# Third convolution of a graph network: marks and hat planes kept in PSUM, with one plane buffer

## The chip, the cores and the metric

The kernel runs on one NeuronCore of a Trainium2 chip. The metric is the device time of one execution in microseconds. It is one program with all its data in that core's HBM at the start; nothing is exchanged with other cores.

## The reference, cut to what matters

A graph of 12,500 nodes and 200,000 edges goes through two blocks, a spline network with three spline convolutions and an attention layer with a gated update. The change touches the third spline convolution alone, the last line of `_L0_gnn_ref`:

```python
def spline_basis(pseudo):                      # pseudo: [E, 3] in [0, 1]
    pos = pseudo * (KS - 1)                    # KS = 5 knots a dimension
    i0 = jnp.clip(jnp.floor(pos), 0, KS - 2).astype(jnp.int32)
    frac = pos - i0
    basis = jnp.prod(jnp.where(combos[None] == 1, frac[:, None, :], 1.0 - frac[:, None, :]), axis=-1)
    ...
def spline_conv(x, row, col, basis, idx, W, b):
    z = jnp.einsum('ni,kio->nko', x, W).reshape(N * K, Fout)       # K = 125
    msg = jnp.einsum('es,eso->eo', basis, z[col[:, None] * K + idx])
    out = jax.ops.segment_sum(msg, row, num_segments=N)
    ...
new_pseudo = jnp.clip(pseudo + t[col] - t[row], 0.0, 1.0)
basis2, idx2 = spline_basis(new_pseudo)
return spline_conv(x, row, col, basis2, idx2, conv_w, conv_b)      # x: 32 features in, 32 out
```

## The kernel before, in words

The program is a chain of phases with a barrier between each two: loading, counting, sorting the edges by source node, a first convolution, the second convolution `flow_conv("c2", ...)`, the third `flow_conv("c3", ...)`, a norm, and the attention. One function, `flow_conv`, builds the second and the third; its argument `moved` is None for the second and the table of node moves for the third. The page and the trace leave buffer and phase numbers out, so both show as `c_...`; the gather from `hid_table` is the second's, the one from `feat_table` the third's.

In the third convolution a node's edges lie together in the array `rows` in HBM, and the nodes are taken in 98 blocks of 128. A block has two halves, `q` = 0 and 1, and a half has 16 windows of 4 nodes. A window is 128 rows of `rows` from where its nodes' edges start. Four strands run side by side, each in its own order:

- **GpSimd (POOL)** fills `rows`. It gathers 128 rows of `feat_table` at a time with an indirect DMA (L961, 1568 of them), whose row numbers it reads from `at` in SBUF; after each four it stores a slot of four tiles to `rows` (L968, 392 stores) and after 16 it copies the next 16 columns of numbers (L956). It never waits for the consumers below.
- **SyncE (SP)** waits until POOL has stored what the block needs (L1012), then, for each half, until VectorE has finished with that half's buffer (L1017), and issues 16 loads of one window each into `rin[:, q]` (L1022) and one of the block's node moves into `trow[:, q]` (L1026).
- **VectorE (DVE)** works on a half in one chain of 19 instructions (`body`, L1108 on). It subtracts the block's first node (`rel`, L1110), makes the edge's position (`pos`, L1123) and the **mark** (L1090), which for each window has, in each of 4 columns, one where the edge belongs to that node. From marks and moves it makes `tsel` (L1128), reduces it to `tsrc` and corrects `pos`. In between and after stand the eight **spreads** (L1084), each mark times feature for two windows. ScalarE makes the sides of the three hats from `pos` (L663 to L668); then DVE finishes the hats (L1144), multiplies the first two dimensions' hats to the **plane** of 5 x 5 values a window (L1095), and plane by third hat to the **basis**, 125 values a window, in two instructions of 8 windows (L1100).
- **TensorE (PE)** multiplies basis by spread for each window into PSUM (L1222), **ScalarE (ACT)** copies the products to `sums` (L1321), and once in two blocks PE mixes the sums with the weights (L1234) and adds up. ACT takes a half's products before it makes the sides of the next half.

Before the change `mark` and `plane` lie in SBUF and have two buffers, one for each `q`. All of PSUM that the third convolution uses is `acc` (four banks of [125, 512]), `mix` and `back` (a bank each); six of the eight banks of 512 fp32 values.

```python
mark = sb(f"{name}_mark", [P, 2, GW2, WN])
plane = sb(f"{name}_plane", [P, 2, GW2, 5, 5])
basis = sb(f"{name}_basis_sb", [P, 2, GW2, 25, 5])
```

Of the kernel before, what the change touches and what calls it, by code (L numbers as in the profile page):

```python
# [13 lines left out]
P = 128  # L14
# [9 lines left out]
WN = 4  # L24
# [30 lines left out]
GW2 = NW // 2  # L55
# [4 lines left out]
def bc(ap, shape):  # L60
    return ap.to_broadcast(shape)
# [14 lines left out]
def allocators(nc, ctx):  # L76
    def sb(name, shape, dt=F32):
        return ctx.enter_context(nc.sbuf_tensor(name, shape, dt))

    def ps(name, shape, dt=F32):  # L80
        return ctx.enter_context(nc.psum_tensor(name, shape, dt))

    def sem(name):
        return ctx.enter_context(nc.semaphore(name))

    return sb, ps, sem
# [782 lines left out]
def flow_conv(nc, c, d, sem, name, turn, table, width, feats, outs, weight, conv_out, moved):  # L869
# [38 lines left out]
    with nc.Block() as block, ExitStack() as ctx:  # L908
        sb, ps, _ = allocators(nc, ctx)
# [1 line left out]
        at = sb(f"{name}_at", [P, 2, RING, slot], U32)  # L911
        rin = sb(f"{name}_rin", [P, 2, GW2, words])
        rel = sb(f"{name}_rel", [P, GW2])
        mark = sb(f"{name}_mark", [P, 2, GW2, WN])
        plane = sb(f"{name}_plane", [P, 2, GW2, 5, 5])
        basis = sb(f"{name}_basis_sb", [P, 2, GW2, 25, 5])
        spread = sb(f"{name}_spread_sb", [P, 2, GW2, feats, WN])
        sums = sb(f"{name}_sums", [K, feats, 2 * P])
# [124 lines left out]
        def _(dve):  # L1043
# [31 lines left out]
            def body(b, item, q):  # L1075
# [16 lines left out]
                                      ALU.is_equal).then_inc(seq, 1)  # L1092

                def make_plane(h):
                    dve.tensor_tensor(plane[:, q, :, :, :], bc(h[:, :, 0, :].unsqueeze(3), [P, GW2, 5, 5]),  # L1095
                                      bc(h[:, :, 1, :].unsqueeze(2), [P, GW2, 5, 5]), ALU.mult).then_inc(seq, 1)

                def make_basis(h):
                    for w in (slice(0, G), slice(G, GW2)):
                        dve.tensor_tensor(basis[:, q, w, :, :],  # L1100
                                          bc(plane[:, q, w, :, :].rearrange("p g a b -> p g (a b)").unsqueeze(3),
                                             [P, G, 25, 5]),
                                          bc(h[:, w, 2, :].unsqueeze(2), [P, G, 25, 5]), ALU.mult)\
                            .then_inc(basis_made, 1)
                        if w.start == 0:
                            dve.wait_ge(basis_made, m * 2 + 1)
# [5 lines left out]
                if moved is None:  # L1112
                    h = rin[:, q, :, src_word + 4:src_word + 19].rearrange("p w (k j) -> p w k j", j=5)
                    make_plane(h)
                    after_step(1)
                    make_mark()
                    after_step(2)
                    make_basis(h)
                    after_step(3)
                    make_spread(*range(pieces))  # L1120
                    dve.sem_inc(seq, 1)
                    return
# [25 lines left out]
                make_spread(6)  # L1148
                after_step(8)
                make_plane(hat[:, q, :, :, :])  # L1150
                make_spread(7)
                after_step(9)
                make_basis(hat[:, q, :, :, :])

            n = dve.value_load(c.passes[0], min_val=1, max_val=EP // P)
# [737 lines left out]
def gnn(nc, ins, out):  # L1893
# [17 lines left out]
    with ExitStack() as top:  # L1911
# [50 lines left out]
        with ExitStack() as nodes:  # L1962
            sb_n, _, _ = allocators(nc, nodes)
            hid = sb_n("hid", [P, NB, HID])
            phase(conv_of_ones, hid[:, :, :])
            phase(conv_to_hidden, "h1", hid[:, :, :], d.stn1_b, d.hid_table)
            phase(flow_conv, "c2", 0, d.hid_table, HID, HID, HID, d.stn2_w, hid[:, :, :], None)
        c.sum3 = sb("sum3", [P, NB, FEAT])
        phase(flow_conv, "c3", 1, d.feat_table, 36, FEAT, FEAT, d.conv_w, c.sum3[:, :, :], d.move)
        c.elr = sb("elr", [P, NB, 2 * HEADS])  # L1970
        c.x, c.h = sb("x2_sb", [P, NB, FEAT]), sb("h2", [P, NB, FEAT])
# [20 lines left out]
```

## Time and profile before

| what | value |
|---|---|
| median of 3 runs | 11174.09 us (11165.35 to 11177.23) |
| span of the profiled execution | 12528.6 us |
| second convolution, 4040 to 6660 us | 2620 us |
| third convolution while POOL gathers, 6670 to 9092 us | 2422 us, POOL busy 1940.1 |
| third convolution after that, to 9620 us | 528 us, POOL busy 0 |
| attention, 9800 to 12528 us | 2728 us |
| DVE busy over the span | 7716.2 us (62%) |
| POOL busy over the span | 7476.5 us (60%) |

The profiled execution is 1354.5 us longer than the median of the timed runs. Its page therefore tells where instructions stand and how long each takes, and less surely how long a phase takes in a run without the profiler. Groups of instructions are given as count, busy time and mean, and behind a bar the engine's idle time just before them with what ended it.

### The profile page before, as it was taken

Reading aid. Unit: us, or ns where it says so; the run is one execution under the profiler, and the core shown is the slowest. Engines: PE = TensorE matmul, PEld = TensorE weight load, DVE = VectorE, ACT = ScalarE, POOL = GpSimd, SP = SyncE. Lnnn points to the kernel's source line nnn. Section 1 sums busy time; section 2 is a strip of 40 time slices with the busy share of each in tenths; the row PEclk is TensorE's granted clock in tenths of the full one; section 3 lists DMA queues with packets and bytes.
Section 4 is the critical chain, followed back from the end, with each engine's and each line's share of the span. In section 5 each row is a group of like instructions: output and inputs, shape, how many; then the busy total and the mean of one; then the engine's idle time right before and its main releaser. Section 6 shows DMA issues by size and latency. Waiting matters only on the chain. (4 is left out here: it accounts for less than half of the span.)

```text
span 12528.6 us, 178083 instructions
## 1 busy us (share of the span) xinstructions
PE 6505.4 (52%) x38968; PEld 5397.9 (43%) x38968; DVE 7716.2 (62%) x17239; ACT 2933.1 (23%) x8407; POOL 7476.5 (60%) x7456
## 2 busy tenths in 40 slices
PE   3466666666475799999994444545555100000000
PEld 2355555555475677777764434434454100000000
DVE  9844444444498676666664444544576267777777
ACT  0011111111132344344432222322343000000001
POOL 5155555655200888888886888888800566666663
PEclk9966666666698999999997667766777555555555
DMA  1210000000733444444443333333322212221221
GB/s 41 65 36 2 2 2 2 2 2 2 14 41 50 93 93 94 92 94 95 92 93 49 50 51 53 54 50 52 54 42 34 35 49 50 51 50 48 51 54 40
DMA packets 1788557, 605.09 MB, mean 48 GB/s; under 512 B 1595943, under 2 KB 1729575, under 8 KB 1788260
## 3 DMA queue, kind: packets, MB, share of 16 engines
q1 hardware_dynamic: 1078132, 311.05, 12.8%
q0 software_dynamic: 255648, 274.30, 10.7%
q10 hardware_dynamic: 454736, 19.28, 3.0%
q8 instruction: 15, 0.25, 0.0%
q14 instruction: 26, 0.21, 0.0%
HBM read 430.75 MB, written 172.95 MB: 48 GB/s over the span
## 5 line engine op out<-in xcount | busy, mean ns | idle before, releaser
L1222 PE MATMUL c_acc<-c_spread_sb,c_basis_sb 128*125 128x256 f32 (+1 forms) x12544 | 2599.2, 376 | 1502.8 <-issue 655.0
L1222 PEld LDWEIGHTS c_acc<-c_spread_sb,c_basis_sb 128*125 128x125 f32 x12544 | 2266.5, 231 | 1803.5 <-issue 1536.3
L1614 POOL DMA_INDIRECT at_ring<-gat_table,at_place x1568 | 1585.7, 1011 | 1188.5 <-issue 1188.5
L609 POOL DMA_INDIRECT rec<-rk_rec,rk_place x1568 | 1619.3, 1033 | 1110.1 <-DVE rk_place L497 620.7
L1321 ACT ACTIVATE c_sums<-c_acc 125x512 f32<-125x512 f32 (+1 forms) x3136 | 1489.3, 490 | 2258.7 <-PE c_acc L1222 1298.6
L961 POOL DMA_INDIRECT c_ring<-hid_table,c_at x1568 | 1707.1, 1089 | 478.9 <-issue 443.2
L961 POOL DMA_INDIRECT c_ring<-feat_table,c_at x1568 | 1602.7, 1022 | 478.1 <-issue 462.9
L1084 DVE TENSOR_TENSOR c_spread_sb<-c_mark,c_rin 128x512 f32<-128x512 f32 (+1 forms) x3136 | 1745.2, 557 | 60.3
L1871 PE MATMUL gr_hps<-ident,gr_hs 128*32 128x128 f32 x98 | 29.8, 408 | 2473.7 <-issue 2066.3
L492 DVE CUSTOM_DVE_ANT_0 rk_junk_l<-rk_look_ps,rk_hi 128x98 bf16<-128x98 f32 x1568 | 402.2, 257 | 1324.1 <-remote 821.1
L1234 PE MATMUL c_mix<-c_sums,c_w 125*64 125x256 f32 (+1 forms) x9408 | 1037.3, 401 | 187.6 <-issue 133.8
L554 PE MATMUL rk_look_ps<-rk_table,rk_lo_t 128*128 128x98 f32 x3136 | 908.7, 425 | 379.5 <-DVE rk_before L492 327.4
L1871 PEld LDWEIGHTS gr_hps<-ident,gr_hs 128*32 128x32 f32 x98 | 6.4, 109 | 2488.1 <-issue 2078.1
L554 PEld LDWEIGHTS rk_look_ps<-rk_table,rk_lo_t 128*128 128x128 f32 x3136 | 705.4, 292 | 503.3 <-DVE rk_before L492 404.2
L1783 DVE TENSOR_REDUCE at_sums<-at_prod 128x128 f32<-128x5248 f32 x98 | 873.3, 8911 | 24.0 <-issue 14.1
L1234 PEld LDWEIGHTS c_mix<-c_sums,c_w 125*64 125x64 f32 (+1 forms) x9408 | 627.4, 132 | 559.2 <-issue 304.0
L530 PE MATMUL rk_rows_ps<-ident,rk_cols 128*128 128x128 f32 x3152 | 771.1, 390 | 4.7 <-ACT rk_cols L564 4.5
L1110 DVE TENSOR_SCALAR c_rel<-c_rin,first 128x16 f32<-128x16 f32 x392 | 103.3, 264 | 1014.6 <-DMA c_rin<-rows 434.9
L587 ACT ACTIVATE rk_table<-rk_run_ps 128x98 f32<-128x98 f32 x784 | 196.2, 250 | 2173.9 <-PE rk_run_ps L549 1208.1
L530 PEld LDWEIGHTS rk_rows_ps<-ident,rk_cols 128*128 128x128 f32 x3152 | 664.9, 292 | 6.4 <-ACT rk_cols L564 6.4
L1144 DVE SCALAR_TENSOR_TENSOR c_hat<-c_hat,c_sides 128x96 f32<-128x96 f32 x196 | 52.5, 268 | 985.3 <-issue 785.6
L487 DVE SCALAR_TENSOR_TENSOR rk_junk<-rk_rows_ps,src_f,rk_earlier 128x128 bf16<-128x128 f32 (+1 forms) x1568 | 647.2, 413 | 2.0 <-PE rk_rows_ps L530 2.0
(356 smaller groups left out, 10126.9 us busy)
## 6 DMA issues: line engine op xcount, KB each, us to landing
c_rin<-rows SPq DMA_DIRECT2D x3136, 42.0 KB
c_rin<-rows SPq DMA_DIRECT2D x3136, 20.0 KB
rows<-c_ring POOLq DMA_DIRECT2D x392, 128.0 KB
rows<-rk_blank SPq DMA_DIRECT2D x112, 252.0 KB
rows<-c_ring POOLq DMA_DIRECT2D x392, 72.0 KB
rows<-at_ring SPq DMA_DIRECT2D x196, 144.0 KB
rec<-rk_rec,rk_place POOLq DMA_INDIRECT x1568
c_ring<-hid_table,c_at POOLq DMA_INDIRECT x1568
```

The lines of the kernel that those rows point to most:

```text
L487: dve.scalar_tensor_tensor(junk[:, u, j // 2, odd:2 * odd + 1, :], rows[:, u, j - odd:j + 1, :], c.src[:, bass.ds(g * G + j, 1)], earlier[ ...
L492: dve.tensor_tensor_reduce(junk_l[:, u, j, :], look[:, j % 2, 0:NB], hi_hot[:, u, j, :], 1.0, 0.0, ALU.mult, ALU.add, before[:, u, j:j + 1 ...
L530: last = pe.matmul(rows[:, u, j, :], bc(cols[:, u, j:j + 1], [P, P]), c.ident[:, :], start=True, stop=True)
L554: pe.matmul(look[:, j % 2, 0:NB], lo_t[:, u, j, :], table[:, k % 2, :], start=True, stop=True).then_inc(looked, 1)
L609: pool.indirect_dma_start(out=d.rec, out_offset=bass.IndirectOffsetOnAxis(ap=place[:, u, j:j + 1], axis=0), in_=rec[:, u, j, :], in_offset ...
L961: pool.indirect_dma_start(out=ring[:, u, j, :], out_offset=None, in_=table, in_offset=bass.IndirectOffsetOnAxis(ap=at[:, h, u, j:j + 1], a ...
L1084: dve.tensor_tensor(spread[:, q, w, :, :], bc(mark[:, q, w, :].unsqueeze(2), [P, 2, feats, WN]), bc(rin[:, q, w, 0:feats].unsqueeze(3), [P ...
L1222: last = pe.matmul(acc[pp % BANKS][:, (w % 2) * WN * feats:(w % 2 + 1) * WN * feats], basis[:, q, w, :, :].rearrange("p a b -> p (a b)"), ...
L1234: last = pe.matmul(mix[k * outs:(k + 1) * outs, 0:2 * P], wsb[:, f, :], sums[:, f, :], start=(i_f == 0), stop=(i_f == each - 1))
L1321: act.activation(sums[:, :, at:at + 2 * WN].rearrange("p f (k n) -> p k f n", n=WN), acc[pp % BANKS][:, 0:pair].rearrange("p (k f n) -> p ...
L1614: pool.indirect_dma_start(out=ring[:, u, j, :], out_offset=None, in_=d.gat_table, in_offset=bass.IndirectOffsetOnAxis(ap=place[:, u, j:j + ...
L1783: dve.tensor_reduce(sums[:, v, :], prod[:, v, :, :, :].rearrange("p s h f -> p (h f) s"), X, ALU.add)\
```

## The change

In the third convolution `mark` and `plane` are allocated in PSUM, and `plane` loses its dimension of two buffers: both halves of a block write and read the same plane. In the second convolution both stay in SBUF, with one plane as well. No instruction is added, removed or moved on any engine.

```diff
-        mark = sb(f"{name}_mark", [P, 2, GW2, WN])
-        plane = sb(f"{name}_plane", [P, 2, GW2, 5, 5])
+        mark = (sb if moved is None else ps)(f"{name}_mark", [P, 2, GW2, WN])
+        plane = (sb if moved is None else ps)(f"{name}_plane", [P, GW2, 5, 5])
...
                 def make_plane(h):
-                    dve.tensor_tensor(plane[:, q, :, :, :], bc(h[:, :, 0, :].unsqueeze(3), [P, GW2, 5, 5]),
+                    dve.tensor_tensor(plane[:, :, :, :], bc(h[:, :, 0, :].unsqueeze(3), [P, GW2, 5, 5]),
                                       bc(h[:, :, 1, :].unsqueeze(2), [P, GW2, 5, 5]), ALU.mult).then_inc(seq, 1)
...
                         dve.tensor_tensor(basis[:, q, w, :, :],
-                                          bc(plane[:, q, w, :, :].rearrange("p g a b -> p g (a b)").unsqueeze(3),
+                                          bc(plane[:, w, :, :].rearrange("p g a b -> p g (a b)").unsqueeze(3),
                                              [P, G, 25, 5]),
                                           bc(h[:, w, 2, :].unsqueeze(2), [P, G, 25, 5]), ALU.mult)\
```

## Rows read from the trace of the kernel before

**Rows 1.** The page: the span.

```profile
span 12528.6 us, 178083 instructions
```

**Rows 2.** Windows by phase: length, busy us (count) by engine, PEclk, DMA share, GB/s.

```profile
core 0: us, PE busy (x) PEld busy (x) DVE busy (x) ACT busy (x) POOL busy (x), PEclk, DMA share, GB/s
...
6670.00:9092.00 2422.00, 1167.36 (x7224) 966.76 (x7224) 1149.66 (x2812) 680.57 (x2136) 1940.10 (x2056) 0.70 0.33 52
9092.00:9620.00 528.00, 309.83 (x2381) 278.58 (x2382) 374.06 (x917) 229.95 (x696) 0.79 (x1) 0.78 0.24 41
```

**Rows 3.** Groups of instructions by line, third convolution while POOL gathers (6670 to 9092).

```profile
L961 POOL DMA_INDIRECT c_ring<-feat_table,c_at x1568 | 1602.7, 1022 | 478.1 <-issue 462.9 <-DMA rows<-c_ring 11.9 <-DMA c_ring<-feat_table,c_at 2.4
L1084 DVE TENSOR_TENSOR c_spread_sb<-c_mark,c_rin 128x256 f32<-128x256 f32 x1184 | 498.2, 421 | 10.2
L1100 DVE TENSOR_TENSOR c_basis_sb<-c_plane,c_hat 128x1000 f32<-128x1000 f32 x294 | 353.7, 1203 | 23.1
L968 POOL DMA_DIRECT2D rows<-c_ring x391 | 313.1, 801 | 0.7
L1095 DVE TENSOR_TENSOR c_plane<-c_hat 128x400 f32<-128x400 f32 x148 | 85.6, 579 | 18.2
...
L1110 DVE TENSOR_SCALAR c_rel<-c_rin,first 128x16 f32<-128x16 f32 x148 | 42.2, 285 | 213.8 <-DMA c_trow<-move 192.1 <-PE c_acc L1222 12.1 <-issue 9.4
L1144 DVE SCALAR_TENSOR_TENSOR c_hat<-c_hat,c_sides 128x96 f32<-128x96 f32 x148 | 39.7, 268 | 945.0 <-issue 785.6 <-ACT c_hat L668 157.2 <-DVE c_spread_sb L1084 2.1
```

**Rows 4.** Line 961 alone: duration in ns, least, median and most.

```profile
L961 POOL DMA_INDIRECT c_ring<-feat_table,c_at x1568: 941/948/1988, 6669.8 to 9086.6; - x196
```

**Rows 5.** Timeline, start and length in us, around one gather of the third convolution.

```profile
8034.13 2.43 DVE L1100 TENSOR_TENSOR c_basis_sb<-c_plane,c_hat 128x1000 f32<-128x1000 f32 x2
8034.19 1.95 POOL L961 DMA_INDIRECT c_ring<-feat_table,c_at  x1 [0.30 <-issue]
```

**Rows 6.** Timeline of the sorting phase, around two indirect DMAs of POOL.

```profile
1803.00 1.68 POOL L609 DMA_INDIRECT rec<-rk_rec,rk_place  x1 [3.40 <-DVE rk_place L497]
...
1803.75 0.97 DVE L465 TENSOR_TENSOR rk_hi<-ramp_bf,src_hi 128x784 bf16<-128x784 bf16 x1
...
1804.98 0.97 POOL L609 DMA_INDIRECT rec<-rk_rec,rk_place  x1 [0.30 <-issue]
...
1805.09 0.48 DVE L487 SCALAR_TENSOR_TENSOR rk_junk<-rk_rows_ps,src_f,rk_earlier 128x256 bf16<-128x256 f32 x1
```

**Rows 7.** Waits of the SP queue in the third convolution: total, times, longest.

```profile
SPq L1017 <- DVE c_spread_sb L1084: 212.0, 30, 21.5
SPq L1012 <- POOLq L972: 32.4, 1, 32.4
```

**Rows 8.** Timeline of SP: three early halves, and two even ones after POOL's end.

```profile
6731.99 9.39 SPq L1022 DMA_DIRECT2D c_rin<-rows  x16
...
6742.80 11.76 SPq L1022 DMA_DIRECT2D c_rin<-rows  x16
...
6757.20 9.69 SPq L1022 DMA_DIRECT2D c_rin<-rows  x16
...
9302.06 9.02 SPq L1022 DMA_DIRECT2D c_rin<-rows  x16
...
9323.98 9.02 SPq L1022 DMA_DIRECT2D c_rin<-rows  x16
```

**Rows 9.** Groups after POOL's end (9092 to 9620).

```profile
L1110 DVE TENSOR_SCALAR c_rel<-c_rin,first 128x16 f32<-128x16 f32 x48 | 11.2, 234 | 77.0 <-PE c_acc L1222 42.3 <-DMA c_trow<-move 34.7
```

**Rows 10.** DVE groups, form by form, whole span: a PSUM input beside SBUF ones.

```profile
L487 DVE SCALAR_TENSOR_TENSOR rk_junk<-rk_rows_ps,src_f,rk_earlier 128x256 bf16<-128x256 f32 x784 | 376.1, 480 | 0.0
L1748 DVE SCALAR_TENSOR_TENSOR at_score<-at_score 128x160 f32<-128x160 f32 x98 | 31.9, 326 | 16.6 <-issue 13.7
L1722 DVE TENSOR_TENSOR gr_gap<-gr_gap,gr_rz 128x64 f32<-128x64 f32 x49 | 11.0, 225 | 1.7
L1718 DVE TENSOR_TENSOR gr_cand<-gr_gps,gr_gap 128x64 f32<-128x64 f32 x49 | 11.0, 225 | 1.7
```

## The prediction

> **What bounds the kernel now.** The change touches the third convolution alone, so I first look for what sets that phase's length. The windows by phase [rows 2] cut it in two: 2422 us in which POOL gathers and stores, then 528 us without POOL. In the first part POOL's own groups leave no hole: 1602.7 us of gathers with 478.1 us between them, 313.1 us of stores [rows 3], in sum 2393.9 of 2422. A gather is followed by the next 0.30 us later, whatever the others do. So POOL waits for nobody, and is itself stretched only by what makes its instructions longer.
>
> Yet POOL does not set the phase's end: 528 us of work are left when it stops. The consumers take 148 halves of blocks (one L1110 each) in the first part [rows 3], 16.4 us a half, and the other 48 [rows 9] at 11.0 us. SP, which feeds them, waits for POOL once, at the start, for 32.4 us [rows 7]. After POOL's end SP starts an even half's loads at 9302.06 and the next at 9323.98 [rows 8]: 21.9 us a block, or 11 a half, and for that stretch the view of SP's waits is empty. So that part is bound by SP's issues of loads. In the first part SP is slower by itself: 25.2 us between the even halves at 6731.99 and 6757.20, with no wait among them (12.6 a half). From 12.6 to 16.4 it is held by the others: VectorE idles 945.0 us before L1144, that is for ScalarE's hats, of which 785.6 us are put down to no cause the profile shows [rows 3], and SP waits 212.0 us for the spreads [rows 7].
>
> **What the change does to POOL.** Two SBUF operands become PSUM operands: the mark in each spread and in the small L1128, the plane in each basis. The rows show why that can matter to POOL. A gather of this line takes 941 ns at least, 948 in the median and 1988 at most [rows 4]. The long ones lie over VectorE instructions with two SBUF inputs: the gather at 8034.19 starts with a basis and takes 1.95 us [rows 5]. In the sorting phase an indirect DMA at 1803.00, with L465 (two SBUF inputs, 0.97 us) begun inside it, takes 1.68; the next, at 1804.98, lies over L487, whose first input is in PSUM and second in SBUF, and takes its 0.97 [rows 6]. L487 has the very arrangement of memories that spread and basis get.
>
> What POOL loses now is the mean over the median: (1022 - 948) ns x 1568 = 116 us [rows 3, 4]. The instructions with two SBUF inputs that remain are the plane (its inputs are hats, only its output moves, 85.6 us), L1144 (39.7 us), the mark's own making and the positions. Spreads and bases are 498.2 + 353.7 = 852 us of the 977 in the four groups named [rows 3], 87%, so some 100 us of the 116 go. I take 100 us: POOL ends after 2322 us in place of 2422.
>
> The Trainium skill says the same mechanism in "SBUF — State Buffer", section Who interferes with whom: a DVE instruction with at most one SBUF input, outside its two-port modes, leaves GpSimd alone, one with two contends with GpSimd's reads. By that rule, the trace agrees: 1.68 against 0.97 us. The page would change nothing in the sum.
>
> **What that is worth at the phase's end.** POOL's end only changes the pace of the consumers from 16.4 to 11.0 us a half. In 100 us less of the first part 100 / 16.4 = 6.1 halves fewer are done; they are done later in 6.1 x 11.0 = 67 us. Net gain: 100 - 67 = 33 us. What hides the other 67 us is SP's queue of loads.
>
> **What it does to VectorE.** No row of the third convolution has a PSUM input. The nearest rows are two. L1718 (first input in PSUM) and L1722 (both in SBUF) are the same instruction at 64 elements, and both take 225 ns: no cost [rows 10]. L1748 takes 326 ns for 160 elements out of SBUF, L487 480 for 256 elements; at the rate by which a basis goes from 256 elements' 421 ns to 1000 elements' 1203 (1.05 ns an element [rows 3]), L487 should take 326 + 96 x 1.05 = 427. So it has 53 ns more, in which its accumulator is contained. Bounds: 0 to +53 ns an instruction. I take 0, since L1718 is the same operation as ours (TENSOR_TENSOR, fp32 out) and L487 is not. Writing PSUM from VectorE is in no row; I take it as equal too, bounded by the same 53 ns, and below nothing by as much, since nothing excludes a faster write.
>
> At the upper bound 13 instructions a half touch mark or plane (mark, tsel, eight spreads, plane, two bases): 13 x 53 = 0.69 us a half, 135 us over 196 halves. Its cover is the wait before L1110, in which VectorE has nothing to do until the loads land: 77.0 / 48 = 1.6 us a half in the second part [rows 9], 213.8 / 148 = 1.44 in the first [rows 3]. Both exceed 0.69, so it costs nothing as long as the loads are late. If that cover is gone, what counts is the ring through ScalarE, below.
>
> Here the skill has a rule against the change. "VectorE: DVE Perf Modes", section The TRN2 errata, gives 58 cycles of fixed cost to an instruction from SBUF and 120 to one from PSUM. That is at 0.96 GHz an estimate of 65 ns more for each of the 11 readers, about 0.7 us a half, and the sum would still be covered. The pair in rows 10 (225 and 225 ns) does not show it.
>
> **One plane buffer.** Both writes and reads of the plane are VectorE's, in its own order: the next half's plane comes after this half's bases, with fifteen instructions between. No wait is added. Cost nothing; there is no other engine behind it. `mark` keeps two buffers. The two banks that they take are beside `acc`, `mix` and `back`, which PE writes.
>
> **The sum.** 12528.6 - 33 = 12496 us for the profiled execution [rows 1]. The timed median is 1354.5 us below that span. I carry the difference over as it is: 11174.1 - 33 = **11141 us**.
>
> **Rivals.** The profiled run may be paced otherwise than the timed ones, and the 785.6 us without a cause before L1144 are the candidate: if they belong to the profiled run, the consumers go at about SP's own 12.6 us a half, 196 x 12.6 = 2470 us, and POOL's 2422 us are as long as that.
>
> *Rival 1, POOL paces the phase.* Then SP waits for POOL's stores, and all that POOL gains is gained: 100 us, up to 116, giving about 11074 (11058 at the end). For it: POOL has no hole, and 2422 and 2470 are near one another. Against it: SP waits for POOL once in the profile.
>
> *Rival 2, nothing moves.* SP's loads are slow beside POOL (11.8 and 9.4 us for 16 against 9.0 after it [rows 8]). If each gather costs SP a fixed time rather than each microsecond with POOL, the same 1568 gathers, packed closer, cost it the same: the second part gets longer by what the first gets shorter. Time: 11174. For it: SP is the strand without waits. That the change does not do what it says (VectorE's one remaining SBUF input is still the one that blocks POOL) gives the same time; against that stands L487.
>
> *Rival 3, slower.* VectorE's PSUM accesses cost 53 ns each and the ring decides: ScalarE's hats, L1144, a spread, plane, a spread, first basis, PE's products, ScalarE's copies of them, and only then the next half's hats. Four PSUM instructions lie on it: 4 x 53 = 0.21 us a half, 42 us over 196 halves; with all 13 it is 135 us. It decides where the waits before L1110 fall under 0.69 us, that is in a run where the loads come 1 us a half sooner than here. With none of the gain: 11174 + 42 = 11216, at most 11309. For it: VectorE does wait for ScalarE's hats (157.2 us so put down). Against it: L1718.
>
> **How the numbers follow.** What the measurement can tell from no change is about 0.2%, 22 us. The forecast (some 20 to 50 us gained) has 0.34; rival 1 has 0.20; rival 2 and its variant 0.33; rival 3 0.13. Of the forecast's case about an eighth lies under 22 us. Faster: 0.30 + 0.20 = 0.50. Same: 0.33 + 0.04 = 0.37. Slower: 0.13. The range goes from rival 1's bound, 11058, to a little under rival 3's 11216, at 11200; it leaves out most of rival 3 and the edges of the others. Within the likeliest case alone it would be 11124 to 11154.
>
> **What would show each step.** POOL's gathers of `feat_table` should have a mean of about 958 ns instead of 1022, and no long ones over a basis; the first part should be near 2322 us, the second longer (some 54 halves x 11.0 = 595 us). L1084 and L1100 should keep 421 and 1203 ns; if they take 470 and 1250 the reading of L1718 was wrong. SP's time for 16 loads beside POOL tells rival 2: it grows above 9.4 to 11.8 us if the cost goes by gathers. Waits of SP at L1012 would tell rival 1. The forecast fails if POOL's mean does not fall, or if it falls and the phase, 2950 us now, keeps its length.

## The result, and the profile after

The changed kernel takes 11050.23 us (median of 4, 11043.24 to 11052.45) against 11169.72 (median of 4, 11164.12 to 11177.23) for the kernel before: a ratio of 0.9887, 95% interval 0.9873 to 0.9901. It is 119 us faster. That is the size of rival 1 and 3.6 times the 33 us of the forecast; it lies 8 us under the range.

The profile after spans 11046.8 us, as long as a timed run. The profiled execution of before [rows 1] had been 1354 us longer than its timed ones, so the two pages can't be held against one another phase by phase. I therefore ran the kernel before once more for its profile; that one spans 11193.0 us, and is what the rows below are compared with.

> The kernel before, unchanged, for a second profile. The profiled run of before spans 12528.6 us where the timed ones take 11170; that of the change spans 11046.8 where the timed ones take 11050. Theory A (POOL paces the third convolution whenever the profiler does not disturb it): the third convolution is about 2480 us long here instead of 2950, POOL's gathers from feat_table have a mean near 1040 ns, SP waits for POOL at L1012 in most blocks, and POOL ends only some 60 us before the phase. Theory B (the consumers pace before, POOL only the changed kernel): POOL ends 100 us or more before the phase ends, SP waits at L1012 a few times only.

It took 11194.85 us, in one execution; the 14 timed ones beside it took 11161.23 to 11190.89. First the windows of the third convolution while POOL gathers and after it, of this second profile of before; columns are the stretch, its length, busy us (instructions) of PE, PEld, DVE, ACT and POOL, clock, DMA share and GB/s:

```profile
6102.00:8557.00 2455.00, 1297.85 (x9426) 1174.48 (x9426) 1502.93 (x3653) 913.12 (x2781) 1967.67 (x2057) 0.76 0.39 60
8557.00:8607.00 50.00, 26.13 (x193) 23.50 (x193) 31.35 (x77) 18.28 (x57) 1.52 (x2) 0.77 0.26 36
```

and of the changed kernel:

```profile
6094.00:8416.00 2322.00, 1264.48 (x9410) 1141.35 (x9410) 1493.86 (x3652) 918.30 (x2778) 1835.04 (x2057) 0.77 0.39 63
8416.00:8465.00 49.00, 28.54 (x208) 25.94 (x209) 33.48 (x79) 19.48 (x60) 1.26 (x2) 0.78 0.26 38
```

The phase took 2505 us and takes 2371. Where [rows 2] had 528 us of work behind POOL's end, there are 50: in an undisturbed run the consumers keep up with POOL, and the phase ends when POOL ends and the last block is done. 133 of the 134 us of the difference lie in the stretch in which POOL gathers.

POOL's gathers, from the groups by line, before (second profile) and after:

```profile
L961 POOL DMA_INDIRECT c_ring<-feat_table,c_at x1568 | 1637.8, 1045 | 477.9 <-issue 463.3 <-DMA rows<-c_ring 9.4 <-DMA c_ring<-feat_table,c_at 4.3
```

```profile
L961 POOL DMA_INDIRECT c_ring<-feat_table,c_at x1568 | 1509.3, 963 | 477.8 <-issue 471.2 <-DMA rows<-c_ring 4.3 <-DMA c_ring<-feat_table,c_at 1.5
```

Their time fell by 1637.8 - 1509.3 = 128.5 us; the idle time between them is the same to 0.1 us. That is the gain, as nearly as it can be told: 128.5 us of gathers and 134 us of the phase in one profile each (these two executions lie 146 us apart as a whole), 119 us between the medians. Least, median and most of one gather's duration say it too, before and after:

```profile
L961 POOL DMA_INDIRECT c_ring<-feat_table,c_at x1568: 940/971/1962, 6111.6 to 8556.0; - x196
```

```profile
L961 POOL DMA_INDIRECT c_ring<-feat_table,c_at x1568: 940/945/1342, 6103.3 to 8414.7; - x196
```

The gathers of nearly 2 us are gone. What is left of up to 1342 ns I put down to the plane's own making and the other instructions that still read SBUF twice; no run takes them away one by one.

What SP waits for in the third convolution answers [rows 7]; second profile of before, then after (total us, times, longest):

```profile
SPq L1012 <- POOLq L972: 312.7, 88, 32.5
...
SPq L1017 <- DVE c_spread_sb L1084: 2.1, 2, 1.1
```

```profile
SPq L1012 <- POOLq L972: 182.0, 78, 32.4
```

Before, SP waited for POOL's stores in 88 cases, nearly each of the 98 blocks. In the profile that the prediction read it had waited once, and 30 times for the spreads. After, it still waits for POOL 78 times, with 131 us less in all.

What SP does in between is the other half of it. Its loads of two halves, 16 each, while POOL gathers; the profile that the prediction read, then the second of before, then after:

```profile
8001.25 12.12 SPq L1022 DMA_DIRECT2D c_rin<-rows  x16
8016.02 12.84 SPq L1022 DMA_DIRECT2D c_rin<-rows  x16
```

```profile
7322.79 9.17 SPq L1022 DMA_DIRECT2D c_rin<-rows  x16
7333.38 8.86 SPq L1022 DMA_DIRECT2D c_rin<-rows  x16
```

```profile
7321.81 9.01 SPq L1022 DMA_DIRECT2D c_rin<-rows  x16
7332.24 9.11 SPq L1022 DMA_DIRECT2D c_rin<-rows  x16
```

Over the whole stretch the median of such a row is 11.6 us in the first profile and 9.0 in the other two; in the first it is 8.9 as well once POOL has ended. So SP was not slow because POOL gathers; it was slow in that one execution.

VectorE's own instructions answer [rows 3] and [rows 10]; again before, then after:

```profile
L1084 DVE TENSOR_TENSOR c_spread_sb<-c_mark,c_rin 128x256 f32<-128x256 f32 x1568 | 660.4, 421 | 13.5
L1100 DVE TENSOR_TENSOR c_basis_sb<-c_plane,c_hat 128x1000 f32<-128x1000 f32 x392 | 471.5, 1203 | 30.8
L1095 DVE TENSOR_TENSOR c_plane<-c_hat 128x400 f32<-128x400 f32 x196 | 113.3, 578 | 24.1
...
L1090 DVE TENSOR_TENSOR c_mark<-c_rel,window_ramp 128x64 f32<-128x64 f32 x196 | 44.0, 225 | 0.8
```

```profile
L1084 DVE TENSOR_TENSOR c_spread_sb<-c_mark,c_rin 128x256 f32<-128x256 f32 x1568 | 656.1, 418 | 13.5
L1100 DVE TENSOR_TENSOR c_basis_sb<-c_plane,c_hat 128x1000 f32<-128x1000 f32 x392 | 470.0, 1199 | 30.8
L1095 DVE TENSOR_TENSOR c_plane<-c_hat 128x400 f32<-128x400 f32 x196 | 114.8, 586 | 24.0
...
L1110 DVE TENSOR_SCALAR c_rel<-c_rin,first 128x16 f32<-128x16 f32 x196 | 50.6, 258 | 543.9 <-DMA c_trow<-move 404.7 <-PE c_acc L1222 139.1
L1090 DVE TENSOR_TENSOR c_mark<-c_rel,window_ramp 128x64 f32<-128x64 f32 x196 | 45.9, 234 | 0.6
```

Reading an operand from PSUM costs nothing: 418 against 421 ns, 1199 against 1203. Writing there costs 8 or 9 ns an instruction (586 against 578, 234 against 225). And before L1110 VectorE still idles 543.9 / 196 = 2.8 us a half: 2.1 of it for the loads (404.7 us), 0.7 for PE's products (139.1 us).

### The profile page after: what moved, and what is told of

The parts are those of the page before. It is cut to its first block and busy times, and to the rows that moved or that the text cites. A ratio compares the mean times of both kernels' runs of the same rounds, so it can differ in the third digit from the quotient of the medians.

```text
span 11046.8 us, 178083 instructions
## 1 busy us (share of the span) xinstructions
PE 5874.2 (53%) x38968; PEld 5015.0 (45%) x38968; DVE 7686.5 (70%) x17239; ACT 3014.7 (27%) x8407; POOL 7464.6 (68%) x7456
## 5 line engine op out<-in xcount | busy, mean ns | idle before, releaser
L1614 POOL DMA_INDIRECT at_ring<-gat_table,at_place x1568 | 1654.5, 1055 | 701.0 <-issue 700.7
L961 POOL DMA_INDIRECT c_ring<-feat_table,c_at x1568 | 1509.3, 963 | 477.8 <-issue 471.2
L1110 DVE TENSOR_SCALAR c_rel<-c_rin,first 128x16 f32<-128x16 f32 x392 | 99.2, 253 | 1285.7 <-DMA c_rin<-rows 643.4
L1234 PE MATMUL c_mix<-c_sums,c_w 125*64 125x256 f32 (+1 forms) x9408 | 867.0, 380 | 24.6 <-ACT c_sums L1321 24.6
L554 PE MATMUL rk_look_ps<-rk_table,rk_lo_t 128*128 128x98 f32 x3136 | 692.2, 354 | 2.0 <-DVE rk_before L492 1.9
L1234 PEld LDWEIGHTS c_mix<-c_sums,c_w 125*64 125x64 f32 (+1 forms) x9408 | 543.1, 128 | 313.5 <-ACT c_sums L1321 34.7
L549 PE MATMUL rk_run_ps<-rk_hi,rk_lo 128*128 128x98 bf16 x1568 | 236.1, 241 | 808.4 <-ACT rk_table L587 808.4
L530 PE MATMUL rk_rows_ps<-ident,rk_cols 128*128 128x128 f32 x3152 | 653.2, 342 | 0.0
L487 DVE SCALAR_TENSOR_TENSOR rk_junk<-rk_rows_ps,src_f,rk_earlier 128x128 bf16<-128x128 f32 (+1 forms) x1568 | 647.0, 413 | 2.4 <-PE rk_rows_ps L530 2.4
L956 POOL COPY c_at<-dst_at 128x16 uint32 (+1 forms) x196 | 59.5, 304 | 859.8 <-POOLq L1930 859.0
L968 POOL DMA_DIRECT2D rows<-c_ring x784 | 626.7, 799 | 15.6 <-DMA c_ring<-hid_table,c_at 9.3
L1774 DVE TENSOR_TENSOR at_prod<-at_weight,at_run 128x1280 f32<-128x1280 f32 x392 | 583.8, 1489 | 10.1
```

What stands on the lines that cost most here:

```text
L487: dve.scalar_tensor_tensor(junk[:, u, j // 2, odd:2 * odd + 1, :], rows[:, u, j - odd:j + 1, :], c.src[:, bass.ds(g * G + j, 1)], earlier[ ...
L530: last = pe.matmul(rows[:, u, j, :], bc(cols[:, u, j:j + 1], [P, P]), c.ident[:, :], start=True, stop=True)
L554: pe.matmul(look[:, j % 2, 0:NB], lo_t[:, u, j, :], table[:, k % 2, :], start=True, stop=True).then_inc(looked, 1)
L961: pool.indirect_dma_start(out=ring[:, u, j, :], out_offset=None, in_=table, in_offset=bass.IndirectOffsetOnAxis(ap=at[:, h, u, j:j + 1], a ...
L968: pool.dma_start(rows_v[:, bass.ds(t * tiles + u * slot, slot), :], ring[:, u, :, :]).then_inc(stored[u], 16)
L1234: last = pe.matmul(mix[k * outs:(k + 1) * outs, 0:2 * P], wsb[:, f, :], sums[:, f, :], start=(i_f == 0), stop=(i_f == each - 1))
```

## The experiments

Ratios are against the kernel before on the same chip in the same session, where its median was between 11180 and 11208 us; that of the change itself is from the result, against 11169.72.

**Which operand brings it.** In the first kernel the mark alone lies in PSUM, in the second the plane alone, in the third neither, so that only the second plane buffer is gone:

```diff
-        plane = (sb if moved is None else ps)(f"{name}_plane", [P, GW2, 5, 5])
+        plane = sb(f"{name}_plane", [P, GW2, 5, 5])
```

```diff
-        mark = (sb if moved is None else ps)(f"{name}_mark", [P, 2, GW2, WN])
+        mark = sb(f"{name}_mark", [P, 2, GW2, WN])
```

(the third has both edits)

> Mark in PSUM, plane in SBUF (one buffer). Theory A, in which each instruction with two SBUF inputs holds up the gathers that begin under it, and longer instructions more: the spreads are many and short (421 ns), the bases are few and long (1203 ns); of the 119 us gained the mark has 20 to 55, so about 11130 us. Rival: the gain comes from the single plane buffer or from the plane alone, then 11170; or each microsecond of such instructions counts the same (spreads 58% of the time), then 70 us, 11100.

> Plane in PSUM (one buffer), mark in SBUF. Theory A: 65 to 100 of the 119 us, about 11085 us. Rival by busy time (bases 42% of it): 50 us, 11120.

> Both in SBUF, with one plane buffer: the part of the change that is not the move. Theory A: same as before, 11170 within 10 us. Rival (the single buffer brings the gain, or costs a stall): 11050, or over 11190.

| in PSUM | ratio to before (95%) | us of 11180 |
|---|---|---|
| mark | 0.9967 (0.9953 to 0.9981) | -37 |
| plane | 0.9915 (0.9899 to 0.9932) | -95 |
| neither, one plane | 1.0002 (0.9992 to 1.0011) | +2 |
| both (the change) | 0.9887 (0.9873 to 0.9901) | -126 |

The parts add up, 37 + 95 = 132 against 126 (each known to some 16 us), and the single buffer is worth nothing beyond the 10 us that its interval leaves. By busy time the bases have 42% of the two (471.5 of 471.5 + 660.4 us), by effect 72%: the same microsecond of VectorE holds POOL up more when it comes in one instruction of 1.2 us than in three of 0.4. POOL's gathers follow; mark alone, plane alone, neither:

```profile
L961 POOL DMA_INDIRECT c_ring<-feat_table,c_at x1568 | 1605.3, 1024 | 477.8 <-issue 464.8 <-DMA rows<-c_ring 7.0 <-DMA c_ring<-feat_table,c_at 5.2
```

```profile
L961 POOL DMA_INDIRECT c_ring<-feat_table,c_at x1568 | 1537.3, 980 | 478.0 <-issue 464.0 <-DMA rows<-c_ring 8.5 <-DMA c_ring<-feat_table,c_at 4.6
```

```profile
L961 POOL DMA_INDIRECT c_ring<-feat_table,c_at x1568 | 1628.1, 1038 | 477.9 <-issue 463.3 <-DMA rows<-c_ring 7.9 <-DMA c_ring<-feat_table,c_at 5.8
```

Against the 1637.8 us of before, that is 32.5, 100.5 and 9.7 us less of POOL, for 37, 95 and about 0 us of time (the last says how far two profiles can differ by themselves).

Why length counts can be read from the trace of the kernel with the mark alone, in which the bases still read SBUF twice and the spreads do not. Three pairs of bases, each with the gathers beside it:

```profile
6377.93 2.43 DVE L1100 TENSOR_TENSOR c_basis_sb<-c_plane,c_hat 128x1000 f32<-128x1000 f32 x2
6378.07 1.88 POOL L961 DMA_INDIRECT c_ring<-feat_table,c_at  x1 [0.32 <-issue]
6380.25 0.94 POOL L961 DMA_INDIRECT c_ring<-feat_table,c_at  x1 [0.30 <-issue]
...
6490.63 2.44 DVE L1100 TENSOR_TENSOR c_basis_sb<-c_plane,c_hat 128x1000 f32<-128x1000 f32 x2
6491.27 1.41 POOL L961 DMA_INDIRECT c_ring<-feat_table,c_at  x1 [0.30 <-issue]
...
6688.06 2.44 DVE L1100 TENSOR_TENSOR c_basis_sb<-c_plane,c_hat 128x1000 f32<-128x1000 f32 x2
6689.52 1.82 POOL L961 DMA_INDIRECT c_ring<-feat_table,c_at  x1 [0.30 <-issue]
```

The first gather begins 0.14 us after its pair and ends 2.02 after the pair's start; the second begins at 0.64 and ends at 2.05. Over the 108 gathers that begin between 0.04 and 0.95 us after a first basis, this end lies between 2.01 and 2.06 us, wherever they began. A gather under a basis is thus held nearly until that basis is done and then takes its own 0.94 us; what it loses is what is left of the instruction. The second basis, which starts 1.23 us after the first, does the same to a gather that begins under it (1.46 after the pair's start, 1.82 us long). But no gather is held by both: none is longer than 1961 ns, though a pair lasts 2.43.

**Which place the PSUM operand has.** Both inputs of spread and basis are swapped:

```diff
-                        dve.tensor_tensor(spread[:, q, w, :, :], bc(mark[:, q, w, :].unsqueeze(2), [P, 2, feats, WN]),
-                                          bc(rin[:, q, w, 0:feats].unsqueeze(3), [P, 2, feats, WN]), ALU.mult)\
+                        dve.tensor_tensor(spread[:, q, w, :, :], bc(rin[:, q, w, 0:feats].unsqueeze(3), [P, 2, feats, WN]),
+                                          bc(mark[:, q, w, :].unsqueeze(2), [P, 2, feats, WN]), ALU.mult)\
```

(and so in the basis)

> The changed kernel with the two inputs of each spread and each basis swapped, so that the PSUM operand is the second and the SBUF operand the first. Theory A (a gather is held up by a VectorE instruction that has two inputs in SBUF, whichever place they have): as the changed kernel, 11050 us within 10. Rival (what counts is that the first input is in PSUM): the gain is lost in part or whole, up to 11170.

Ratio 0.9878 (0.9861 to 0.9896), gathers of 962 ns in the mean: as the change. Either input may be the one in PSUM.

**The suspected cost by itself.** One instruction of 1024 elements is added to the changed kernel after each half's bases; nobody uses its result. Only its first input differs between the two kernels:

```diff
                 make_basis(hat[:, q, :, :, :])
+                dve.tensor_tensor(extra[:, :, :], bc(c.ramp[:, 64:128].unsqueeze(1), [P, 16, 64]),
+                                  bc(c.ramp[:, 0:64].unsqueeze(1), [P, 16, 64]), ALU.mult)
```

```diff
                 make_basis(hat[:, q, :, :, :])
+                dve.tensor_tensor(extra[:, :, :], bc(mark[:, q, :, :].rearrange("p g r -> p (g r)").unsqueeze(1), [P, 16, 64]),
+                                  bc(c.ramp[:, 0:64].unsqueeze(1), [P, 16, 64]), ALU.mult)
```

> The changed kernel with one VectorE instruction more after each half's bases, 1024 elements, both inputs in SBUF, result used by nobody; 196 x 1.22 us = 240 us more VectorE work. Theory A: 392 bases with two SBUF inputs cost 95 us (plane alone moved: 11180 to 11085), 0.24 us each; 196 of these cost 48 us (35 to 75): about 11098 us, with POOL's gather mean near 990 ns instead of 963. Rival 1 (VectorE's time is on the path): some of the 240 us, and as much in the next kernel. Rival 2: nothing, 11050.

> The same extra instruction, but its first input is the mark in PSUM. Theory A: VectorE waits 2.8 us a half for its loads in the changed kernel, over 1.22, so nothing is added: 11050 to 11060 us, POOL's gather mean 963 ns. Rival (VectorE's time on the path): as long as the kernel with two SBUF inputs.

With both inputs in SBUF the ratio is 0.995 (0.9933 to 0.9968), with one in PSUM 0.9881 (0.9864 to 0.9899): 0.0069 x 11190 = 77 us between two kernels that do the same amount of work on VectorE. POOL's gathers, two SBUF inputs first:

```profile
L962 POOL DMA_INDIRECT c_ring<-feat_table,c_at x1568 | 1581.2, 1008 | 477.8 <-issue 464.2 <-DMA rows<-c_ring 6.7 <-DMA c_ring<-feat_table,c_at 6.1
```

```profile
L962 POOL DMA_INDIRECT c_ring<-feat_table,c_at x1568 | 1507.7, 962 | 477.8 <-issue 469.0 <-DMA rows<-c_ring 5.2 <-DMA c_ring<-feat_table,c_at 2.7
```

They differ by 1581.2 - 1507.7 = 73.5 us. So 240 us more of VectorE's time cost nothing where POOL was let alone, and 77 us where each instruction read SBUF twice. I had expected 48 us (35 to 75); an instruction that stands alone costs 77 / 196 = 0.39 us, while a basis, one of two back to back, costs 95 / 392 = 0.24. The rows of the pairs above show why a pair costs less than two: a gather held by the first basis is through before the second is, and the next one (at 6380.25) begins in the last 0.11 us of the pair and is not held. Counted over that trace, the gathers that begin under a first basis take 62.6 us more in all than 942 ns each, those that begin under a second 37.1.

**How far the cover reaches.** Three such instructions with the mark in PSUM instead of one:

```diff
                 make_basis(hat[:, q, :, :, :])
+                for x in range(3):
+                    dve.tensor_tensor(extra[:, x, :, :], bc(mark[:, q, :, :].rearrange("p g r -> p (g r)").unsqueeze(1), [P, 16, 64]),
+                                      bc(c.ramp[:, 0:64].unsqueeze(1), [P, 16, 64]), ALU.mult)
```

> The changed kernel with three extra instructions after each half's bases, 1024 elements each, first input the mark in PSUM, results used by nobody: 3 x 1.22 = 3.66 us a half more for VectorE, where one such instruction (1.22 us) cost nothing. Theory A (POOL paces until the consumers' slack, 2.8 us a half before L1110, is used up): 0.9 us a half above the slack, 196 x 0.9 = 170 us more than 11050, 11220 us (11100 to 11350), POOL's gather mean still 963 ns and POOL's end well before the phase's. Rival (the slack is larger, because VectorE also waits for ScalarE, 0.7 us a half before L1144): 11050 to 11100.

Ratio 0.9981 (0.9972 to 0.9991), that is (0.9981 - 0.9887) x 11187 = 105 us over the change; inside the range expected, under its middle. The windows, the gathers and SP's waits of this kernel (the last 40 us of the second window are already the next phase's):

```profile
6095.00:8412.00 2317.00, 1216.65 (x8977) 1098.95 (x8977) 2028.60 (x4026) 882.87 (x2645) 1828.04 (x2058) 0.74 0.42 62
8412.00:8620.00 208.00, 96.41 (x728) 86.37 (x728) 169.86 (x300) 67.77 (x199) 0.00 (x0) 0.72 0.23 35
```

```profile
L962 POOL DMA_INDIRECT c_ring<-feat_table,c_at x1568 | 1500.6, 957 | 478.0 <-issue 467.7 <-DMA rows<-c_ring 5.5 <-DMA c_ring<-feat_table,c_at 4.0
```

```profile
SPq L1018 <- DVE c_spread_sb L1085: 263.2, 189, 2.2
SPq L1013 <- POOLq L973: 35.0, 2, 32.6
```

POOL is as fast as in the change and done at 8412, and then 160 us of VectorE's chain are left (its last basis starts at 8572.4; in the change at 8462.6, 110 us earlier). The three instructions kept VectorE busy 680.8 us, 3.47 a half, and cost 105 / 196 = 0.54, so the room was 2.9 us a half: nearly all of the 2.8 before L1110 (543.9 us in the change, 48.0 left here), and a little before L1144 (143.4 us, 100.1 left). VectorE is busy 2028.60 of 2317 us, and SP waits for it 189 times and for POOL twice. This is what a phase paced by its consumers looks like here: work behind POOL's end and no waits at L1012. The profile that the prediction read had work behind POOL's end too, and one wait for POOL; but there SP's own loads were slow, and it waited for VectorE only 30 times.

**The same cure elsewhere.** The second convolution is built by the same function, and all eight banks are used in it. The kernel below frees one by letting the third layer's products use the bank of the transposes, which they never meet in time, and puts one buffer of marks and one of planes there. `flow_conv` builds both convolutions, so the third now has a single buffer of marks as well; its gathers stay as they are (944 ns in the median, at most 1334):

```diff
-        mark = (sb if moved is None else ps)(f"{name}_mark", [P, 2, GW2, WN])
-        plane = (sb if moved is None else ps)(f"{name}_plane", [P, GW2, 5, 5])
+        hats = ps(f"{name}_hats", [P, 512])
+        mark = hats[:, 0:GW2 * WN].rearrange("p (g r) -> p g r", r=WN)
+        plane = hats[:, GW2 * WN:GW2 * (WN + 25)].rearrange("p (g a b) -> p g a b", a=5, b=5)
...
-            turn_ps, deep_ps = ps("mt_turn_ps", [P, 512]), ps("mt_deep_ps", [P, 512])
+            turn_ps = ps("mt_turn_ps", [P, 512])
+            deep_ps = turn_ps
```

> Marks and planes of the second convolution in PSUM as well: one bank holds one buffer of each (64 + 400 values), and the bank comes from letting the third layer's products share the bank of the transposes, which are never in flight with them. In the second convolution POOL has no hole either and its gathers have a mean of 1095 ns. Theory A: they fall to about 965, 130 x 1568 = 205 us, if PE (busy 2322 of 2625 us there) does not pace the phase first; 11050 - 205 = 10845 at best, 10950 if PE takes half. Rival (PE or the loads pace the second convolution already): 11050.

It takes 10842.93 us, ratio 0.9686 (0.9669 to 0.9704). The gathers of the second convolution in the changed kernel and in this one, and the windows of that phase:

```profile
L961 POOL DMA_INDIRECT c_ring<-hid_table,c_at x1568 | 1717.5, 1095 | 478.8 <-issue 447.2 <-DMA rows<-c_ring 17.0 <-DMA c_ring<-hid_table,c_at 13.7
```

```profile
L963 POOL DMA_INDIRECT c_ring<-hid_table,c_at x1568 | 1508.5, 962 | 478.4 <-issue 456.2 <-DMA rows<-c_ring 17.1 <-DMA c_ring<-hid_table,c_at 4.3
```

```profile
3470.00:6095.00 2625.00, 2322.09 (x13418) 1793.04 (x13418) 1755.93 (x2748) 1073.93 (x2057) 2064.27 (x2058) 0.94 0.44 92
```

```profile
3490.00:5884.00 2394.00, 2239.45 (x13418) 1736.24 (x13418) 1754.99 (x2748) 1064.37 (x2057) 1835.48 (x2058) 0.98 0.52 101
```

209 us less of POOL, and by the ratios (0.9887 - 0.9686) x 11190 = 225 us of time, although PE shows busy in 2239 of the 2394 us that are left (at a granted TensorE clock of 0.98, against 0.94). Its busy share is no limit here.

At last, on top of that kernel, the attention's softmax weights, first input of the products (392 instructions of 1489 ns), go to PSUM, a bank for each buffer:

```diff
-        weight = sb("at_weight", [P, 2, RUN + 1, HEADS])
+        weight_ps = ps("at_weight", [P, 2, 512])
+        weight = weight_ps[:, :, 0:(RUN + 1) * HEADS].rearrange("p v (s h) -> p v s h", h=HEADS)
```

> The kernel with the second convolution moved too, and in the attention the softmax weights (first input of the products at_prod, 392 instructions of 1489 ns with two SBUF inputs) in PSUM, a bank for each of two buffers. Theory A: POOL's gathers from gat_table have a mean of 1054 ns against 943 to 963 where nothing holds them up, so up to 100 ns x 1568 = 155 us of its time goes; POOL gathers ahead only in that phase's first part, whose blocks VectorE also paces, so between 50 and 150 us of it show: about 10745 us. Rival (VectorE, 76% busy in the attention, paces it): 10843, as without.

It takes 10674.69 us (10672.85 to 10677.94), ratio 0.9527 (0.9511 to 0.9543): 4.7% under the kernel before, and better than both kernels of this case. The gathers from `gat_table` in the changed kernel and in this one:

```profile
L1614 POOL DMA_INDIRECT at_ring<-gat_table,at_place x1568: 940/945/2237, 8645.9 to 10891.9; - x196
```

```profile
L1617 POOL DMA_INDIRECT at_ring<-gat_table,at_place x1568: 941/947/1093, 8439.4 to 10518.6; - x196
```

None is over 1093 ns any more, and the stretch in which they stand is 2246 us long before and 2079 after. So POOL paces that phase too, nearly alone: its gathers take 1487.3 us in place of 1652.2, 165 less, and 168 us lie between the medians of this kernel and the one above, 178 us by the ratios ((0.9686 - 0.9527) x 11195). I had put the top at 150.

## Why the prediction was wrong, point by point

**POOL's loss was read rightly, and a bit small.** The prediction took 116 us of loss and 100 of gain; it was 128.5. The profile it read had 148 of the 196 halves beside POOL; the other 48 came after POOL's end and could not hold it up. In a run in which all 196 lie beside POOL, the same 100 us are 100 x 196 / 148 = 132. This alone puts the bound of rival 1 at 11174 - 116 x 196 / 148 = 11020 and not at 11058, and would have held the result in the range.

**The step that failed is "What that is worth at the phase's end".** It took the paces 16.4 and 11.0 us a half from the profiled execution and let 67 of 100 us go to SP's loads. The second profile of before has no such pace: 196 halves in 2505 us, 12.8 us each, 50 us of work behind POOL, SP's loads at 9.0 us and not 11.6 while POOL gathers, and 88 waits of SP for POOL. Nothing of the 67 us is hidden: the gathers lose 128.5 us and the phase 134. Where POOL paces, every microsecond taken off it is one off the phase. Rival 1 had said so.

**The sum then carried the disturbance over.** "The timed median is 1354.5 us below that span. I carry the difference over as it is" treats the 12% of unexplained time as lying outside the paces that the sum used. It lay in them too: the third convolution takes 2950 us in the first profile and 2505 in the second. So it was elsewhere, but not everywhere: the last indirect DMA of the sorting phase starts at 3253.6 and at 2687.2 us, what follows the third convolution takes 2908 and 2586, and the second convolution 2620 and 2622. The sign was on the page: 785.6 us of idle time before L1144 without a cause [rows 3]. In the second profile VectorE's idle time at this line is 207.9 us, all of it put down to ScalarE's hats:

```profile
L1144 DVE SCALAR_TENSOR_TENSOR c_hat<-c_hat,c_sides 128x96 f32<-128x96 f32 x196 | 53.0, 271 | 207.9 <-ACT c_hat L668 207.9
```

The prediction named this idle time as the reason for rival 1 and then gave it 0.20, less than the case that took the disturbed pace at face value. What slowed that one profiled execution is open (its granted TensorE clock in the stretch was 0.70 against 0.76, which may be cause or consequence). All later ones, of ten other kernels and of before itself, span within 0.3% of their timed runs.

**What was right.** An input in PSUM stops VectorE from holding POOL up, as L487 had shown [rows 6]. Reading PSUM costs nothing, as the pair of L1718 and L1722 said [rows 10]; the 53 ns by which L487 is longer do not come with an input in PSUM. By an estimate from the Trainium skill's 58 and 120 cycles ("VectorE: DVE Perf Modes", The TRN2 errata) the spreads would have become 65 ns longer; they are 3 ns shorter. The Trainium skill's rule that two SBUF inputs contend with GpSimd's reads and one does not ("SBUF — State Buffer", Who interferes with whom) holds in each of the runs, with a number that the page does not give: 0.39 us for each lone instruction of 1.2 us. Writes to PSUM, in no row before, cost 8 or 9 ns, within the bound of 53. One plane buffer cost nothing (1.0002).

**A reading that was off without harm.** The cover for a slower VectorE was taken as time "until the loads land", 77.0 / 48 = 1.6 us a half. Of these 77.0 us only 34.7 are put down to the loads, 0.72 us a half, and 42.3 to PE's products [rows 9]. The forecast took 0 for the accesses, so nothing hung on it.

**The rivals.** Rival 2 (each gather costs SP a fixed time, so nothing moves) is out: SP waits for POOL, and its 16 loads take 9.0 us beside POOL before and after. Its variant, that one SBUF input still blocks, is out by the gathers' mean (963 ns), and in either place of the operand by the swap. Rival 3 is out: nothing that reads PSUM got slower, and writes by 8 or 9 ns. That VectorE can take the phase over is real, but needs far more than its 0.69 us a half: at 3.47 more it does.

## What to carry to other kernels

Where GpSimd issues indirect DMAs back to back and paces a phase, look at the longest of them against their median, and at the VectorE instructions over which they lie: those with two SBUF inputs, and the long ones first. Moving one small, often read operand of them to a spare PSUM bank took that time off GpSimd in three phases of this program and cost VectorE next to nothing. Before an estimate is made from the pace of a phase, hold the profiled span against the timed median; where they are 12% apart, idle time without a cause is the profile's own suspect, and the case without it is the likelier one.

## What the hardware showed that I had not expected

- A gather that begins under an instruction of VectorE with two SBUF inputs loses what is left of that instruction, and the next instruction in line does not hold it again. So length counts for more than VectorE's total: 660 us of spreads cost POOL 32.5 us, 471 us of bases 100.5.
- PE shows busy for 2322 of 2625 us in the second convolution, and still the phase gets 231 us shorter when POOL does (2239 of 2394).
- One profiled execution of a kernel can be 12% longer than its timed ones, with one phase of the program untouched (2620 against 2622 us) and its neighbour 18% longer (2950 against 2505).
